# Modulation weights as the moving operand in four column tiles, and a reordered opening, in a transformer block on one Trainium2 core

## What is computed

```python
e = emb[:, 0, :]                       # 16 conditions of 512
gb = e @ w.T + b                       # w: 1024 x 512, one w per stage
gamma, beta = jnp.split(gb, 2, axis=-1)
xn = (x - mu) * jax.lax.rsqrt(var + EPS)
return xn * (1.0 + gamma[:, None, :]) + beta[:, None, :]
```

```python
x = res + attn(rope(xn1 @ Wq), rope(xn1 @ Wk), xn1 @ Wv) @ Wo
x = res + attn(rope(xn2 @ Wq2), rope(ctx @ Wk2), ctx @ Wv2) @ Wo2
x = res + (gelu(xn3 @ W1 + b1) @ W2 + b2)
```

## Time and profile before

| | |
|---|---|
| median of 3 runs | 2095.88 us |
| the profiled execution | 2100.82 us |
| its span (first to last instruction) | 2098.8 us |
| PE busy | 2034.9 us, 97% |
| DVE, ACT, POOL busy | 51%, 49%, 41% |
| first head's scores on PE | 77.09 us |

### The profile page before, as it was taken

How to read it: one execution, slowest core, us unless ns; L and a number is a source line. 1 busy time by engine, 2 the same in 40 slices (tenths; PEclk the granted TensorE clock), 3 DMA queues, 4 the chain that set the end, 5 groups by cost and what they waited for, 6 DMA issues and landing times. The chain is left out here.

```text
span 2098.8 us, 37400 instructions
## 1 busy us (share of the span) xinstructions
PE 2034.9 (97%) x13632; PEld 1686.8 (80%) x13632; DVE 1076.0 (51%) x1940; ACT 1037.9 (49%) x1858; POOL 864.0 (41%) x946
## 2 busy tenths in 40 slices
PE   6799999999999999999999999799999999999999
PEld 6688888888887788888888887578888888888887
DVE  4555766767766776666667667443222222222211
ACT  2344665666665666666666666643233232323322
POOL 1344565665656577676676666510110101011010
PEclk9788999999999999999999999999999999999999
DMA  4665666665677666667667668241010101101010
GB/s 162 187 173 156 181 179 169 181 187 169 175 196 199 188 191 203 191 175 207 190 172 212 189 176 234 71 156 52 10 61 1 60 21 41 60 1 60 1 41 20
DMA packets 239346, 277.93 MB, mean 132 GB/s; under 512 B 13888, under 2 KB 194368, under 8 KB 239168
## 3 DMA queue, kind: packets, MB, share of 16 engines
q1 hardware_dynamic: 239168, 275.55, 45.4%
HBM read 183.23 MB, written 92.27 MB: 131 GB/s over the span
## 5 line engine op out<-in xcount | busy, mean ns | idle before, releaser
L796 POOL TENSOR_TENSOR sums_sb<-prob 128x256 f32<-128x256 f32 x512 | 403.4, 793 | 337.2 <-ACT prob L635 335.7
L739 DVE TENSOR_REDUCE neg_max<-ps_s 128x2 f32<-128x512 f32 x512 | 347.1, 686 | 326.5 <-PE ps_s L515 324.2
L635 ACT ACTIVATE prob<-ps_s 128x512 f32<-128x512 f32 x512 | 304.7, 596 | 363.8 <-PE ps_s L535 358.1
L1094 DVE TENSOR_TENSOR h_lo<-h_sb,h_hi 128x512 fp32r<-128x512 f32 x128 | 92.4, 722 | 515.0 <-ACT h_hi L1055 515.0
L1051 ACT ACTIVATE h_sb<-ps_h,b_sb 128x512 f32<-128x512 f32 x128 | 88.2, 689 | 490.7 <-PE ps_h L994 490.7
L515 PE MATMUL ps_s<-kT,qT 96*128 96x256 f32 x1024 | 227.0, 303 | 4.1 <-DVE neg_max L739 2.8
L790 POOL TENSOR_TENSOR rope_c<-rope_c,rope_s 128x512 f32<-128x512 f32 x128 | 178.5, 1395 | 124.4 <-DVE rope_s L718 123.6
L535 PE MATMUL ps_s<-qT,kT 104*128 104x256 f32 x1024 | 210.3, 288 | 14.6 <-ACT qT L627 9.8
L515 PEld LDWEIGHTS ps_s<-kT,qT 96*128 96x128 f32 x1024 | 167.2, 192 | 67.6 <-issue 52.0
L505 PE MATMUL ps_g<-xx_hi,w_hi 128*128 128x256 f32 x1024 | 214.0, 291 | 5.5 <-issue 5.5
L505 PE MATMUL ps_g<-xx_hi,w_lo 128*128 128x256 f32 x1024 | 209.8, 287 | 0.0
(11 more groups left out here) (114 smaller groups left out, 4381.1 us busy)
## 6 DMA issues: line engine op xcount, KB each, us to landing
kT<-k_turned SPq DMA_DIRECT2D x192, 256.0 KB, 4.5
qT<-q_turned SPq DMA_DIRECT2D x64, 512.0 KB, 6.5
k_turned<-rot_hi SPq DMA_DIRECT2D x64, 256.0 KB, 4.2
k_turned<-rot_lo SPq DMA_DIRECT2D x64, 256.0 KB, 4.0
q_turned<-rot_hi SPq DMA_DIRECT2D x64, 256.0 KB, 2.4
q_turned<-rot_lo SPq DMA_DIRECT2D x64, 256.0 KB, 2.4
qT<-q_turned SPq DMA_DIRECT2D x64, 256.0 KB, 6.9
xn<-in_x SPq DMA_DIRECT2D x16, 512.0 KB, 3.7
```

The lines of the kernel that those rows point to most:

```text
L635: eng.activation(prob[:, n % NP, :, :].rearrange("p t l -> p (t l)"), ps_s[:, score_bank(step), :], ACT.Exp, scale=HD ** -0.5).then_inc(ex ...
L739: eng.tensor_reduce(neg_max[G % 2][:, :, j], ps_s[:, score_bank(step), :].rearrange("p (t l) -> p t l", l=L), AX.X, ALU.max, negate=True). ...
L796: eng.tensor_tensor(sums_sb[:, n % NP, :], prob[:, n % NP, 0, :], prob[:, n % NP, 1, :], ALU.add).then_inc(halves_added, 1)
L1094: eng.tensor_tensor(h_lo[a % NH][:, :], h_sb[a % 2][:, :], h_hi[a % NH][:, :].bitcast(F32), ALU.subtract).then_inc(h_lo_done, 1)
```

## The change

Four things are done.

The conditions become the stationary operand and the modulation weights the moving one. For half h of the 1024 outputs (the scales or the shifts) four matmuls, one to a chunk c of the contraction, write 32 partitions each of one bank, in the column tile at partition 32 c. Of each 32 weight columns, 16 are the conditions of the chunk and 16 are those of the next one (or zeros), whose result isn't used. The four partial sums are copied to SBUF by ACT (`mod_copy`), turned by four transposes on PE (`mod_turn`) and added up with the bias by four DVE operations (`mod_add`). Each half takes two of the rotating banks.

The opening is in another order: the six casts of `pick` come first on DVE; the modulation weights are loaded ahead of the k weights; the small inputs are issued by ACT instead of SP; the k weights are split after `turn_x` instead of before the modulation; item 1 is normalised and turned beside the first projections of item 0; splitting of v and o weights is spread out; v of item 0 is projected last, behind k of item 1.

The split of the four rows of output weights moves into the first item of the loop (places 4, 8, 12 and 16).

The modulation of the second and third stage is placed as four halves, one in each of items 0 to 3, instead of four quarters each in items 0 and 1.

```diff
     for i in range(-1, N):
         p, ahead = 48 * i, i + 2
-        if 0 <= i < 2:
-            put(p + 24, "mod_load", i + 1, 0)
-            put(p + 24, "mod_load", i + 1, 1)
+        if 0 <= i < 4:
+            n, h = 1 + i // 2, i % 2
             for c in range(KC):
-                put(p + 44 + c, "mod", i + 1, c)
-                if c + 2 < KC:
-                    put(p + 44 + c, "mod_load", i + 1, c + 2)
+                put(p + 20 if i == 0 else p - 14, "mod_load", n, h, c)
+            for k, kind in enumerate(("mod", "mod_copy", "mod_turn", "mod_add")):
+                put(p + 30 + k, kind, n, h)
...
+    for c, row in enumerate(rows["o"]):
+        put(4 * c + 4, "w_split", *row)
+    yield ("pick",)
+    for h in range(2):
+        yield ("mod_load", 0, h, None)
     for row in rows["k"]:
         yield ("w_load", *row)
-    for c in range(KC):
-        yield ("mod_load", 0, c)
     for t in range(T):
         yield ("stats", 0, t)
     yield ("norm", 0)
     for t in range(T):
         yield ("scale", 0, t)
-    for before, after in zip(rows["k"], rows["q"]):
-        yield ("w_split", *before)
-        yield ("w_load", *after)
-    for c in range(KC):
-        yield ("mod", 0, c)
+    for h in range(2):
+        for kind in ("mod", "mod_copy", "mod_turn", "mod_add"):
+            yield (kind, 0, h)
     for half in range(2):
         yield ("turn_x", 0, half)
-    for half in range(2):
-        yield ("x_high", 0, half)
-        yield ("x_low", 0, half)
-    for before, after in zip(rows["q"], rows["v"]):
-        yield ("w_split", *before)
-        yield ("w_load", *after)
+
+    def split(m, cs, after=None):
+        for c in cs:
+            yield ("w_split", *rows[m][c])
+            if after:
+                yield ("w_load", *rows[after][c])
+
+    def rotated(m, t):
+        for kind in ("rope_high", "rope_low", "spill"):
+            yield (kind, m, 0, t)
+        if t == 0:
+            yield ("stack", m, 0)
+
+    yield ("x_high", 0, 0)
+    yield ("x_low", 0, 0)
+    yield from split("k", (0, 1), "q")
+    yield ("x_high", 0, 1)
+    yield ("x_low", 0, 1)
+    yield from split("k", (2, 3), "q")
+    early = [step for place in sorted(places) if place < -24 for step in places.pop(place)]
+    turns_of_x = ("turn_x", "x_high", "x_low")
+    yield from (step for step in early if step[0] not in turns_of_x)
     yield from project("k", 0, 0)
+    yield from split("q", (0, 1), "v")
+    yield from rotated("k", 0)
+    yield from (step for step in early if step[0] in turns_of_x)
     yield from project("k", 0, 1)
-    for before, after in zip(rows["v"], rows["o"]):
-        yield ("w_split", *before)
-        yield ("w_load", *after)
-    for m, after in ("kq", "qv"):
-        for t in range(T):
-            yield ("rope_high", m, 0, t)
-            yield ("rope_low", m, 0, t)
-            yield ("spill", m, 0, t)
-            if t == 0:
-                yield ("stack", m, 0)
-        if m == "k":
-            yield ("pick",)
-        for t in range(T):
-            yield from project(after, 0, t)
-    for row in rows["o"]:
-        yield ("w_split", *row)
+    yield from split("q", (2, 3), "v")
+    yield from rotated("k", 1)
+    for t in range(T):
+        yield from project("q", 0, t)
+        yield from split("v", (2 * t, 2 * t + 1), "o")
+        yield from rotated("q", t)
+    yield ("b1_load",)
     for place in sorted(place for place in places if place < 0):
         yield from places.pop(place)
+    for t in range(T):
+        yield from project("v", 0, t)
...
+            first_mods = [[prob_row[:, c * D:(c + 1) * D] for c in range(KC)],
+                          [prob_row[:, (KC + c) * D:(KC + c + 1) * D] for c in range(2)] + [sums_row[:, c * D:(c + 1) * D] for c in range(2)]]
+            first_in = [[sem(f"first_mod_in{h}{part}") for part in range(2)] for h in range(2)]
+            mod_parts = [sums_row[:, 2 * D:3 * D], w_raw[:, 0, :], w_raw[:, 0, :]]
...
+                return mod_added, KC * nth[old]
...
-                        n, c = step[1:]
-                        if n == 0 and c == 0:
+                        n, h = step[1:]
+                        if n == 0 and h == 0:
                             eng.wait_ge(small_in["cond"], 16)
-                        if n:
-                            slot, loads = raw_turn["mod_load", n, c]
-                            eng.wait_ge(raw_in[slot], 16 * loads)
-                            row = w_raw[:, slot:slot + 2, :].rearrange("p a d -> p (a d)")
-                        else:
-                            eng.wait_ge(first_in[c], 16)
-                            row = first_mods[c]
-                        b = bank(("mod", n, 0))
-                        for m in range(2 * KC):
-                            ins = eng.matmul(ps_g[:, b, m * B:(m + 1) * B], row[:, m * P:(m + 1) * P], cond_sb[:, c, :],
-                                             start=c == 0 and m == 0, stop=c == KC - 1, skip_group_check=True)
+                            eng.wait_ge(cond_padded, 1)
+                        for c in range(KC):
+                            if n:
+                                slot, loads = raw_turn["mod_load", n, h, c]
+                                eng.wait_ge(raw_in[slot], 16 * loads)
+                                row = w_raw[:, slot, :]
+                            else:
+                                eng.wait_ge(first_in[h][c // 2], 16)
+                                row = first_mods[h][c]
+                            ins = eng.matmul(ps_g[c * 2 * B:(c + 1) * 2 * B, bank(step), :], cond_sb[:, c * B:(c + 2) * B], row,
+                                             start=True, stop=True)
                         ins.then_inc(mod_done, 1)
+                    elif kind == "mod_turn":
+                        n, h = step[1:]
+                        if n == 0 and h == 0:
+                            eng.wait_ge(small_in["ident"], 16)
+                        eng.wait_ge(mod_copied, nth[step])
+                        for k in range(KC):
+                            ins = eng.transpose(ps_g[:, bank(step), k * P:(k + 1) * P], mod_parts[n][:, k * P:(k + 1) * P], ident[:, :])
+                        ins.then_inc(mod_turned, 1)
...
+                for s in range(2):
+                    eng.dma_start(pick_sb[ROWS + s * OH:ROWS + (s + 1) * OH, :], pick[0:OH, 0:OH]).then_inc(small_in["pick"], 16)
+                eng.dma_start(ident[:, :], ident_in).then_inc(small_in["ident"], 16)
+                eng.dma_start(ln_b[:, :, :], lnb).then_inc(small_in["lnb"], 16)
+                eng.dma_start(cos_sb[:, :], cos).then_inc(small_in["cos"], 16)
+                eng.dma_start(sin_sb[:, :, :], sin).then_inc(small_in["sin"], 16)
...
+                    elif kind == "mod_copy":
+                        n, h = step[1:]
+                        eng.wait_ge(mod_done, nth[step])
+                        if h:
+                            eng.wait_ge(mod_turned, nth[step] - 1)
+                        eng.activation(mod_parts[n], ps_g[:, bank(("mod", n, h)), :], ACT.Copy).then_inc(mod_copied, 1)
...
-                    elif kind == "mod" and step[2] == KC - 1:
-                        n = step[1]
-                        if n == 0:
+                    elif kind == "mod_add":
+                        n, h = step[1:]
+                        if n == 0 and h == 0:
                             eng.wait_ge(small_in["lnb"], 16)
-                        eng.wait_ge(mod_done, nth[step])
-                        eng.tensor_tensor(gb[:, n, :, :],
-                                          ps_g[:, bank(("mod", n, 0)), 0:2 * KC * B].rearrange("p (m b) -> p m b", b=B),
-                                          ln_b[:, n, :].unsqueeze(2).broadcast_to([P, 2 * KC, B]), ALU.add).then_inc(mod_added, 1)
-                        eng.wait_ge(mod_added, n + 1)
-                        eng.tensor_scalar(gb[:, n, 0:KC, :], gb[:, n, 0:KC, :], 1.0, None, ALU.add).then_inc(gb_ready, 1)
+                        eng.wait_ge(mod_turned, nth[step])
+                        mine = gb[:, n, h * KC:(h + 1) * KC, :]
+                        of_chunk = ps_g[:, bank(("mod_turn", n, h)), :].rearrange("p (k c b) -> p c k b", c=KC, b=2 * B)
+                        before = ln_b[:, n, h * KC:(h + 1) * KC].unsqueeze(2).broadcast_to([P, KC, B])
+                        for c in range(KC):
+                            if c:
+                                eng.wait_ge(mod_added, KC * (nth[step] - 1) + c)
+                            ins = eng.tensor_tensor(mine, of_chunk[:, c, :, 0:B], mine if c else before, ALU.add)
+                            ins.then_inc(mod_added, 1)
+                        if h == 0:
+                            eng.wait_ge(mod_added, KC * nth[step])
+                            eng.tensor_scalar(mine, mine, 1.0, None, ALU.add).then_inc(gb_ready, 1)
...
+                        source = lnT[n, :, h * D:(h + 1) * D].rearrange("(c p) d -> p c d", p=P)
```

(9 more changed lines are left out.)

54 lines of the change are left out of this document (24 added, 30 removed).

## The result

The changed kernel took 2071.26 us (median), the kernel before 2096.43 us beside it: a ratio of 0.9871, 95% interval 0.9847 to 0.9895. It is faster, by 25 us where I forecast 40; the forecast of 2056 us was 15 us too low, and the time lies near the upper end of the range (2044 to 2072). One of the four runs took 4998.07 us, with full-width matmuls on PE at half the pace or less; nothing is drawn from it, and the profile here is of a later execution (2073.35 us), whose set gave 0.9877 (0.9861 to 0.9894).

What follows compares the result with a forecast made beforehand. PE, busy 97%, was taken to bound the kernel. Loop 19 us (28.5 less 5.5 less 4) plus opening 24 less 3 given back makes 40 us, so 2056 us was forecast, with a range of 2044 to 2072.

Steps and rivals of the forecast that it cites:

- removed in the loop: Old modulation on PE in the loop: 22.3 us own time, less 1 overlapping, plus 7.2 of half pace, 28.5 us gained.
- own price of the halves: Four loop halves on PE: matmuls 0.88 us and transposes 0.5 each, 1.4 us a half, 5.5 us added.
- waits that the halves add: PE in the loop waits for ACT's copy, 0.3 us a half, and for banks, 1 us three times: 4 us, 0 to 12.
- first scores sooner: Opening: new order starts the first scores at 53 us instead of 77.09, 24 us sooner; bounds 49 and 62.
- given back: PE's wait for the stack with half pace behind it, and output weights split on DVE in item 0: 3 us, 0 to 7.
- rival D: First items: PE waits for DVE and the clock falls behind each wait; over 11 further waits make it slower; chance 0.02.
- change of tile width: Drain of PE at each switch of tiling mode, twice a half: 1.5 us less gain, judged against by the trace.
- Removal of the low clock: Loop: the half-pace stretches around the old modulation go, 7.2 us; sign: no stretch of 0.50 around 110 or 170 us.
- C: Loop: clock answers to the new matmuls as to the old, four low stretches of 15.4 us, 2092 us; chance 0.04.
- E: Modulation matmuls: tiles don't run beside one another, 1.9 instead of 0.88 us a half, 2061 us; chance 0.08.
- A: Opening is bound by transfers, not by order; first scores at 62 us, 2065 us in all; chance 0.18.
- B: Every wait counted as new is hidden, stack, copies and banks cost nothing: 2046 us; chance 0.16.

Runs made afterwards that it cites:

- late_add: Changed kernel with only the additions of each loop half moved two places later (33 to 35), the transposes left in place: 2060.46 us, ratio 0.9827 to the kernel before.
- late_turn: Changed kernel with the transposes (32 to 34) and the additions (33 to 35) of each loop half two places later: 2054.68 us, ratio 0.9799 to the kernel before.
- o_early: Changed kernel with the four rows of output weights split in the opening, as before, instead of in item 0: 2074.89 us, ratio 0.9903 to the kernel before.
- twice_matmuls: late_turn with each loop half's four 512-column matmuls done twice over, writing the same values: 2058.67 us, ratio 0.9822 to the kernel before.
- old_mod_new_order: New order of the opening and output weights split in item 0, with the modulation as in the kernel before: 2081.88 us, ratio 0.9933 to the kernel before.
- q_split_first: late_turn with all q weights split ahead of item 1's turning and the modulation's loads shifted: 2053.78 us, ratio 0.9802 to the kernel before.

## Why the prediction was right in sign and kind, and 15 us off

| step | forecast | measured |
|---|---|---|
| removed in the loop | 28.5 | 27.4 |
| own price of the halves | -5.5 | -5.5 (four times 0.99 and 0.38) |
| waits that the halves add, with the clock behind them | -4 | -18.4 (23.9 less 5.5) |
| first scores sooner | 24 | 20.0 |
| given back | -3 | -0.5 to head 0; what follows to head 6 is in the halves |
| behind head 58 | 0 | 3.9 |
| sum | 40 | 27 |

**The step that failed** is the one that adds the waits: "0.3 us a half" for the copy, "1 us each" for the bank, 4 us in all and 12 at the most, where 18.4 were measured. The mechanisms were the right ones, but were sized by the length of what each engine does, not by the place in the list at which it gets to it. I let ACT be, at worst, busy with an exponential. In fact it was idle in front of one, whose scores stood on PE behind the very matmuls, and the copy came after: 1.05 us of idle four times, and 6.8 us by late_add against late_turn. For the bank I counted DVE's additions and products, but not that DVE would start on them only behind the reduction of scores that PE issues behind the turn: 1.69, 1.92 and 1.69 us. Two waits weren't in the sum at all: 1.8 us for the weights of the first half, and POOL's sums behind the first additions (2.15 us, where the kernel before waits 1.14).

**The price left out** is the clock behind these waits. I had the pattern, in rival D (1.89 us, then 3.4 us at 0.50), and charged none of it to a half. The second and third half each have such a stretch (half of 3.4, 1.7 us), the fourth has none, and costs 4.8 us against 6.4 and 6.6. In o_early the second and the fourth have one and cost 6.4 us each, the third has none and costs 5.1. By the trace 4.2 of the 18.4 us are the copies, 5.3 the bank, 1.8 the weights, 1.0 POOL's sums, 3.9 the low clock up to head 58 and 0.8 the change of tile width, of which below; 1.4 stay without a name. D itself did not come true: it needed more than 11 waits with a fall behind them, and there were three in the loop (falls at 92.1, 129.6 and 174.0) and two in the opening (37.4 and 57.9).

**Removal of the low clock** held. I had named a low clock at any half as the sign of C, and three halves have one; but C is refuted by 1.00 from 109.3 to 126.4 us, with the second half's matmuls in it, and by late_turn and twice_matmuls, in which no half has a low stretch; E by the further quartets.

**The change of tile width** costs about what I had put in a rival case, though I read the rows against it. The Trainium skill (TensorEngine Tiling (Array Packing), Key Properties) says that a change of the tiling mode drains the engine. I set the end of the narrow group, 181.04, against it, but the profile models the ends of matmuls; the starts tell otherwise. The pair of full-width matmuls right behind the second half's narrow group takes 0.35 us (121.96 to 122.31), the next pair 0.23. A half's first quartet takes 0.99 us, a further one of twice_matmuls 0.86. And the first narrow matmul starts 0.21 us behind the full-width one ahead of it, where full-width ones start 0.12 apart. Together it is 0.3 us a half and 1.3 for four, near the 1.5 that I had priced; 0.13 of it a half is in the 0.99 above. So the starts agree with the page in that each change costs time; whether it is a drain no run here shows.

**The opening** followed the forecast with each stage somewhat late: `xT` 1.4 us, the scores 4.1. At `xT` the second half's quartet ran whole behind the first half's turn (12.76 to its copy at 14.76), where I had counted its last pair alone, 0.9 us. Then q's first product starts on DVE at 41.18, 5 us later than I had: DVE splits q's last two rows only from 36.35 to 39.37, behind ACT, which turns to them after item 1's x. PE waits 2.52 us for them and goes on at 0.50; late_turn has no low stretch there and starts the same product at 41.08, so the clock is little of it. Spill and stack then took what I had: second spill issued at 45.72, stack at 50.50 (4.8 us, forecast 4.4), scores 6.6 us behind. So A has the last wait right (it is for `qT`), but the lateness arose ahead of the transfers, and its 62 us weren't reached; B is refuted for this kernel. That only 0.5 us are given back to head 0 is partly luck: the wait of 1.89 us at 88.45 and its 3.4 us at 0.50 went, and 6.8 us at 0.50 behind the first scores came (the first stretch above). That late_turn lands at 2054.7, close to the forecast, is luck as well: there the waits happen to cost 4.5 us (10.0 less 5.5), what I had assumed of the kernel as written, and 5.6 us behind head 58, which I hadn't forecast, stand in for the 4 that the opening is short.

**Not settled**: behind head 58 all kernels gain 3 to 5.6 us on the kernel before, old_mod_new_order too (17.0 to 20.5). Most of it, 2.6 to 3.6 us, falls between heads 220 and 240 (652 to 714 us of the kernel before). Before has two short stretches at 0.50 there, the changed kernel one, late_turn none; but q_split_first has as much as before and gains 3.0 us too. No edit stands there, and what brings this isn't shown.

## What to carry to other kernels

Where all engines walk one list, a step's wait is sized from the list and not from durations: look at what each engine must first pass to reach its part, and whether that waits for something which the engine you want to spare issues later. Put a chain PE, ACT, PE, DVE at distances at which each engine has already passed its neighbours; here two numbers in one line, with no instruction changed, were worth 16 to 18 us of 2073. And a wait of 1.7 to 2.2 us on a PE that is otherwise full is priced with the fall of the clock that may follow it: here 1.7 us more, in 7 of 12 cases.
